# Ternary weight pieces shared between two engines, and TensorE's filler loads left out, in an eight-core FFN-attention-FFN kernel

## The chip, the cores and the metric

The kernel runs on the 8 NeuronCores of one Trainium2 chip, one batch element of 4096 rows of 1024 numbers on each core. The cores share no data. The metric is the device time in microseconds of the slowest core.

## The reference, cut to what matters

```python
# layer 0 (macaron)
x = x + 0.5 * ffn(layernorm(x), w_gate, w_up, w_down)
x = x + attn(layernorm(x), Wq1, bq1, Wk1, bk1, Wk2, bk2, Wproj, bproj)
x = x + 0.5 * ffn(layernorm(x), w_gate, w_up, w_down)

def weight_quant(w):               # one scale per matrix
    scale = 1.0 / clip(mean(abs(w)), 1e-05)
    return clip(round(w * scale), -1.0, 1.0) / scale

def ffn(x, w_gate, w_up, w_down):  # 1024 -> 4096 -> 1024
    gate = silu(act_quant(x) @ weight_quant(w_gate).T)
    up = act_quant(x) @ weight_quant(w_up).T
    return act_quant(gate * up) @ weight_quant(w_down).T

def attn(V, ...):                  # elementwise, with running sums over the rows
    K = exp(V @ Wk1.T + bk1);  Q = sigmoid(V @ Wq1.T + bq1)
    O_ar = cumsum(K * V) / (cumsum(K) + 1e-6) * Q
    ...
    return (O_ar + O_ma) @ Wproj.T + bproj
```

## The kernel before, in words

**Ternary weights.** The three FFN matrices (16 MB each in float32) are turned into matrices of -1, 0 and 1 in bf16, once, and kept in device memory (`sc_g`, `sc_u`, `sc_d`). `emit_tern_stream` does it one matrix after the other, in two passes each. The mean pass (`tern_mean`, `mean_piece`) loads 16 pieces of 128 x 2048 and ScalarE sums their absolute values (L237); `mean_finalize` makes a scale of it. The write pass (`tern_write_gu`, `tern_write_d`) loads the 16 pieces again, and `tern_piece` works on each: two DVE operations over 2048 elements scale and clamp it (L291, L294), then four times two operations over 512 elements add a large constant while converting to int32 (L301) and subtract it while converting to bf16 (L304). That rounds. POOL's queue then issues the store (L310).

Pieces go through four load buffers (`tpc`) and four store buffers (`tst`), chosen by `bsel`, the running number of the piece modulo 4. SP issues all piece loads (L231), in order, each when the last user of its buffer is done (`slotV`). A new mean pass on ScalarE starts when DVE has done all it was given up to there (`cV.wait(S)` in `tern_mean`).

**The main loop.** It takes 8 chunks of 512 rows. For each: the first FFN (`emit_ffn_rest`), attention (`emit_attn`), then the second FFN. The gate and up weights are loaded in slices by ScalarE's queue (`gu_load`, L549 and L551), the first two right before the matmuls of L602 and L607. Transposes come before the matmuls, rounded out of PSUM by DVE (L420, L425) or ScalarE (L436, L440) in turn.

**Attention's end.** The elementwise chain (`chain(th)`) is done for the two halves of a chunk, th = 0 and 1, in four lanes of two column blocks: lanes 0 and 1 on DVE, 2 and 3 on POOL with scans on DVE. `wproj_mms(th)` multiplies its result with Wproj on TensorE: four bias matmuls (L1022), then eight matmuls of 128x512 for each lane (L1037), which wait for the lane and for the lane's pair of weight blocks (`dAW`, loaded by POOL's queue, L734). `te_fill(n)` puts n weight loads of 128x128 without a matmul (L1013) into TensorE's queue: 140 at the start of a half, 50 ahead of each later lane's wait. `wproj_evac(th)` adds the result to the chunk on DVE (L1055). The order of emission, and so of each engine's queue, is: `chain(0)`, `wproj_mms(0)`, `chain(1)`, `wproj_evac(0)`, a part of the layer norm statistics, `wproj_mms(1)`, `wproj_evac(1)`, and then the second FFN's quantising and transposes.

Of the kernel before, what the change touches and what calls it, by code (L numbers as in the profile page):

```python
# [10 lines left out]
AF = mybir.ActivationFunctionType  # L11
ALU = mybir.AluOpType
# [28 lines left out]
def build_nc(L=4096, T=512):  # L41
# [21 lines left out]
    if DEBUG_ATTN:  # L63
# [20 lines left out]
    aq = poolb[:, 0:4096].rearrange("p (a b c) -> p a b c", a=TT, b=DC)  # L84
# [21 lines left out]
    qiV = qi32[:, 0:512]  # L106
    qiS = qi32[:, 512:1024]
# [30 lines left out]
    nm128_ap = smal[:, 187:188]  # L138
    dcol = smal[:, 143:144]
# [16 lines left out]
    cV = Sem(st, nc, "cV")  # L156
    cS = Sem(st, nc, "cS")
# [3 lines left out]
    V, S, TE, SY, G = nc.vector, nc.scalar, nc.tensor, nc.sync, nc.gpsimd  # L161
# [24 lines left out]
                           scalar1=-2.0, scalar2=-1.0,  # L186
                           op0=ALU.add, op1=ALU.mult))
    cV.wait(V)
    V.tensor_scalar(out=dcol, in0=t1[:, 0:1], scalar1=MAGIC, scalar2=None,
                    op0=ALU.mult)  # L190
    cV.inc(V.tensor_scalar(out=nm128_ap, in0=t1[:, 0:1], scalar1=-MAGIC,
                           scalar2=None, op0=ALU.mult))
    dB.inc(SY.dma_start(out=bsb[:, 0:DC],
                        in_=bq1.ap().rearrange("(j p) -> p j", p=128),
                        allow_slow_non_contiguous=True), 16)
    dB.inc(SY.dma_start(out=bsb[:, DC:2 * DC],
                        in_=bk1.ap().rearrange("(j p) -> p j", p=128),
                        allow_slow_non_contiguous=True), 16)
    dB.inc(SY.dma_start(out=bsb[:, 2 * DC:3 * DC],
                        in_=bk2.ap().rearrange("(j p) -> p j", p=128),  # L200
# [7 lines left out]
                           op0=ALU.mult))  # L208
    dX[0].inc(SY.dma_start(out=xsb[0][:, :, :],
                           in_=x_hbm.ap()[0:T, :]  # L210
# [8 lines left out]
    tw_state = {"idx": 0, "slotV": [None] * 4, "stgV": [None] * 4}  # L219

    def tern_dma_in(src_ap, pf):
        i = tw_state["idx"]
        tw_state["idx"] += 1
        bsel = i % 4
        buf = tpc[bsel][:, 0:pf]
        if tw_state["slotV"][bsel] is not None:
            sem_, n_ = tw_state["slotV"][bsel]
            SY.wait_ge(sem_.h, n_)
        else:
            cV.wait(SY)  # L230
        dTI[bsel].inc(SY.dma_start(out=buf, in_=src_ap), 16)  # L231
        return bsel, buf
# [53 lines left out]
    def tern_piece(src_ap, dst_ap, sw_slot, pf, osems, sw_wait=False):  # L286
        bsel, buf = tern_dma_in(src_ap, pf)
        sbf = tst[bsel][:, 0:pf]
        dTI[bsel].wait(V)
        cV.wait(V)  # L290
        cV.inc(V.tensor_scalar(out=buf, in0=buf, scalar1=sw_slot, scalar2=1.4375,  # L291
                               op0=ALU.mult, op1=ALU.min))
        cV.wait(V)
        cV.inc(V.tensor_scalar(out=buf, in0=buf, scalar1=-1.4375,  # L294
                               scalar2=None, op0=ALU.max))
        prev = tw_state["stgV"][bsel]
        if prev is not None:
            prev[0].wait(V, prev[1])
        for j0 in range(0, pf, 512):
            cV.wait(V)  # L300
            cV.inc(V.tensor_scalar(out=qiV[:, 0:512], in0=buf[:, j0:j0 + 512],  # L301
                                   scalar1=dcol, scalar2=None, op0=ALU.add))
            cV.wait(V)
            cV.inc(V.tensor_scalar(out=sbf[:, j0:j0 + 512], in0=qiV[:, 0:512],  # L304
                                   scalar1=nm128_ap, scalar2=None,
                                   op0=ALU.add))
        tw_state["slotV"][bsel] = (cV, cV.n)
        cV.wait(G)
        osem = osems[bsel]
        osem.inc(G.dma_start(out=dst_ap, in_=sbf), 16)  # L310
        tw_state["stgV"][bsel] = (osem, osem.n)

    def tern_write_gu(w_hbm, scratch, sw_slot, osems):
        for ob in range(8):
            for icg in range(2):
                src = bass.AP(w_hbm, icg * 4 * 128 * INNER + ob * 512,
                              [[INNER, 128], [128 * INNER, 4], [1, 512]])
                dst = bass.AP(scratch, ob * (128 * 8 * 512) + icg * 4 * 512,
                              [[8 * 512, 128], [512, 4], [1, 512]])
                tern_piece(src, dst, sw_slot, 2048, osems,  # L320
                           sw_wait=(ob == 0 and icg == 0))

    def tern_write_d(w_hbm, scratch, sw_slot, osems):
        for icg in range(8):
            for h2 in range(2):
                src = bass.AP(w_hbm, (icg * 4 + h2 * 2) * 128 * D,
                              [[D, 128], [128 * D, 2], [1, D]])
                dst = bass.AP(scratch, icg * (128 * 4 * 1024) + h2 * 2 * 1024,
                              [[4 * 1024, 128], [1024, 2], [1, 1024]])
                tern_piece(src, dst, sw_slot, 2048, osems,  # L330
                           sw_wait=(icg == 0 and h2 == 0))
# [388 lines left out]
    def emit_attn(c, xb, pre01_done=False):  # L720
# [8 lines left out]
        def aw_load(w_hbm, k):  # L729
            bs = k % 4  # L730
            G.wait_ge(cT.h, aw_arena_cT[bs])
            src = bass.AP(w_hbm, (k % 4) * 2 * 128 * D,
                          [[D, 128], [128 * D, 2], [1, D]])
            dAW[bs].inc(G.dma_start(  # L734
                out=awb[:, bs * 2048:(bs + 1) * 2048], in_=src), 16)

        def aw_tile(k, et):
            bs = (k // 2) % 4
            off = bs * 2048 + (k % 2) * 1024 + et * 128
            return awb[:, off:off + 128]  # L740
# [267 lines left out]
                cV.inc(V.tensor_copy(out=xnc, in_=xn2T[:, :, 512]))  # L1008
            return lane_done

        def te_fill(n):
            for _ in range(n):
                TE.ldweights(weights=aq[:, 0, 0, :])  # L1013

        def wproj_mms(th, lane_done):
            TE.wait_ge(cV.h, wp_evac_cV[th])
            TE.wait_ge(cS.h, proj_evac_cS[th])
            te_fill(140)
            TE.wait_ge(lane_done[0][0].h, lane_done[0][1])
            for tt in (th * 2, th * 2 + 1):  # L1020
                for eb in range(2):
                    TE.matmul(out=pb[th * 4 + (tt % 2) * 2 + eb][:, :],  # L1022
                              lhsT=onesrb[:, :],
                              rhs=bprow[:, eb * 512:(eb + 1) * 512],
                              start=True, stop=False)
            for dc in range(DC):
                kp = dc // 2
                bsel = kp % 4
                dAW[bsel].wait(TE)
                if dc % 2 == 0:  # L1030
                    if kp > 0:
                        te_fill(50)
                    TE.wait_ge(lane_done[kp][0].h, lane_done[kp][1])
                tl_ = None
                for tt in (th * 2, th * 2 + 1):
                    for eb in range(2):
                        tl_ = TE.matmul(  # L1037
                            out=pb[th * 4 + (tt % 2) * 2 + eb][:, :],
                            lhsT=OB_[:, dc, tt * 128:(tt + 1) * 128],
                            rhs=aw_tile(dc, 0)[:, 0:0 + 512] if False else  # L1040
                            awb[:, bsel * 2048 + (dc % 2) * 1024 + eb * 512:
                                bsel * 2048 + (dc % 2) * 1024 + (eb + 1) * 512],
                            start=False, stop=(dc == DC - 1))
                cT.inc(tl_)
                if dc % 2 == 1:
                    aw_arena_cT[bsel] = cT.n
                    if kp + 2 < 4:
                        aw_load(wpt, kp + 2)
# [24 lines left out]
        if DEBUG_ATTN and c == 0:  # L1073
# [3 lines left out]
                                 in_=pool[:, 8192:12296]), 16)  # L1077
# [9 lines left out]
        aw_load(wpt, 1)  # L1087
        lanes0 = chain(0)
        wproj_mms(0, lanes0)
        aw_load(wpt, 0)  # L1090
        aw_load(wpt, 1)
        lanes1 = chain(1)
        if DEBUG_ATTN and c == 0:
            cV.wait(SY)
            cS.wait(SY)
            for i_, ap_ in enumerate([pool[:, 4096:8192], pool[:, 12296:16392],
# [5 lines left out]
                                    in_=ap_), 16)  # L1102
            dDB.inc(SY.dma_start(out=bass.AP(dbgq, 0, [[4104, 128], [1, 4104]]),
                                in_=poolb[:, 4096:8200]), 16)
            dDB.inc(SY.dma_start(out=bass.AP(dbgq, 128 * 4104,
                                            [[4104, 128], [1, 4096]]),
                                in_=poolb[:, 8200:12296]), 16)
# [3 lines left out]
        wproj_evac(0)  # L1111
        ln_stats_part(xb, (0, 1))
        wproj_mms(1, lanes1)
        wproj_evac(1)

# [6 lines left out]
    for c in range(NCH):  # L1122
        xb = xsb[c % 2]
        if c + 1 < NCH:
            if c >= 1:
                dO.wait(SY, 16 * c)
            dX[(c + 1) % 2].inc(SY.dma_start(
                out=xsb[(c + 1) % 2][:, :, :],
                in_=x_hbm.ap()[(c + 1) * T:(c + 2) * T, :]
# [6 lines left out]
        if c + 1 < NCH:  # L1136
# [6 lines left out]
            out=y_hbm.ap()[c * T:(c + 1) * T, :].rearrange("(a p) d -> p a d",  # L1143
                                                           p=128),
            in_=xb[:, :, :]), 16)
# [29 lines left out]
```

## Time and profile before

| | us |
|---|---|
| timed runs | 6789.29 and 6901.66 (median 6845.48) |
| profiled execution | 6789.22 |
| its span on the slowest core (core 4) | 6788.2 |
| spans of the eight cores | 6708.1 to 6788.2 |
| mean granted TensorE clock of the eight cores | 0.794 to 0.800 of full speed |
| busy on core 4: TensorE, DVE, ScalarE, POOL | 3997.4, 2602.3, 1580.0, 489.5 |

Times in the rows further down are microseconds from the start of core 4's span. PE is TensorE's matmuls, PEld its weight loads, DVE is VectorE, ACT ScalarE, POOL GpSimd, SP the engine that only issues DMAs; ACTq is ScalarE's sequencer, which issues DMAs too. A granted clock of 1.00 is 2.4 GHz, 0.50 is 1.2 GHz.

### The profile page before, as it was taken

How to read it: one execution, taken by the hardware profiler on the slowest of the kernel's cores; microseconds unless marked ns; L12 is line 12 of the kernel's file. 1: busy time of each engine (PE TensorE's matmuls, PEld its weight loads, DVE VectorE, ACT ScalarE, POOL GpSimd, SP SyncE). 2: the span in 40 equal slices, each digit the busy share in tenths (PEclk: the TensorE clock that was granted, in tenths of full speed). 3: DMA queues.
4: the chain of work that ended last, by engine and by line, in shares of the span. 5: the costliest groups of instructions: out<-in, count | busy, mean ns of one | idle time of the engine just before them, and what ended most of it. 6: DMA issues, size and time to landing. Idle time of an engine off the chain costs nothing.

```text
span 6788.2 us, 61510 instructions; the slowest of 8 cores (6708.1 to 6788.2 us)
## 1 busy us (share of the span) xinstructions
PE 3997.4 (59%) x19026; PEld 2319.6 (34%) x23666; DVE 2602.3 (38%) x4295; ACT 1580.0 (23%) x2080; POOL 489.5 (7%) x505
## 2 busy tenths in 40 slices
PE   0006647576377745686376754686475763777457
PEld 0002333344333343334343343333333433333333
DVE  4555343331642244332532325422433315422352
ACT  2111221231131221322131321312213311312212
POOL 0000020001200020000200011000200002000200
PEclk6558868798689867898688877898687986898778
DMA  6784343235224252244233252243432352232522
GB/s 210 241 257 156 73 73 106 75 102 120 46 81 139 84 93 81 64 135 98 51 100 112 90 103 69 68 155 72 73 104 70 104 111 51 87 124 84 94 81 90
DMA packets 229245, 700.29 MB, mean 103 GB/s; under 512 B 22096, under 2 KB 22096, under 8 KB 224848
## 3 DMA queue, kind: packets, MB, share of 16 engines
q10 hardware_dynamic: 110592, 402.70, 19.0%
q0 software_dynamic: 76576, 159.41, 12.8%
q1 hardware_dynamic: 41776, 134.24, 6.4%
q8 instruction: 180, 2.95, 0.2%
q14 instruction: 121, 0.99, 0.1%
HBM read 788.55 MB, written 41.94 MB: 122 GB/s over the span
## 4 chain that ended last, share of the span: by engine, by line
PE 39%; DVE 23%; DMA 15%; ACT 13%; issue 7%; POOL 1%; DVEq 1%; ACTq 0%; SPq 0%; POOLq 0%
PE PB L602 11%; PE PB L607 10%; PE PB L684 9%; DMA sarena<-sc_d 8%; PE PB L754 4%; PE PB L403 4%; DVE pool L572 3%; ACT qi L436 2%; DMA sarena<-sc_u 2%; ACT poolb L440 2%; ACT pool L643 2%; DMA poolb<-wq1t 2%; DVE poolb L304 1%; DVE qi L301 1%; DVE smal L578 1%
## 5 line engine op out<-in xcount | busy, mean ns | idle before, releaser
L602 PE MATMUL PB<-sarena,poolb 128*128 128x512 bf16 x4096 | 1578.9, 385 | 358.8 <-DMA sarena<-sc_u 129.9
L607 PE MATMUL PB<-sarena,poolb 128*128 128x512 bf16 x4096 | 1577.9, 385 | 0.0
L684 PE MATMUL PB<-sarena,poolb 128*128 128x512 bf16 x4096 | 956.0, 391 | 228.6 <-DMA sarena<-sc_d 227.3
L403 PE MATMUL PB<-ident,pool 128*128 128x128 f32 x2144 | 496.6, 368 | 960.1 <-ACT pool L517 367.0
L572 DVE SCALAR_TENSOR_TENSOR pool<-PB,smal,pool 128x512 f32<-128x512 f32 x512 | 381.8, 746 | 1314.0 <-ACT pool L569 1314.0
L403 PEld LDWEIGHTS PB<-ident,pool 128*128 128x128 f32 x2144 | 379.1, 197 | 999.4 <-issue 997.6
L602 PEld LDWEIGHTS PB<-sarena,poolb 128*128 128x128 bf16 x4096 | 405.4, 99 | 921.8 <-issue 478.0
L684 PEld LDWEIGHTS PB<-sarena,poolb 128*128 128x128 bf16 x4096 | 396.2, 100 | 784.2 <-issue 374.1
L569 ACT ACTIVATE pool<-PB,smal 128x512 f32<-128x512 f32 x512 | 326.5, 684 | 1423.0 <-PE PB L607 1391.7
L607 PEld LDWEIGHTS PB<-sarena,poolb 128*128 128x128 bf16 x4096 | 405.3, 99 | 473.4 <-issue 28.7
L754 PE MATMUL PB<-poolb 128*128 128x256 bf16 x3072 | 401.1, 296 | 169.2 <-ACT pool L770 125.5
L697 DVE SCALAR_TENSOR_TENSOR xsb<-PB,smal,xsb 128x512 f32<-128x512 f32 x64 | 43.6, 744 | 1160.4 <-PE PB L684 1160.4
L420 DVE TENSOR_SCALAR qi<-PB,smal 128x512 int32<-128x512 f32 x320 | 240.1, 750 | 432.6 <-PE PB L406 418.2
L754 PEld LDWEIGHTS PB<-poolb 128*128 128x128 bf16 x3072 | 319.7, 106 | 250.8 <-issue 187.7
L1037 PE MATMUL PB<-poolb 128*128 128x512 bf16 x512 | 211.3, 588 | 325.5 <-issue 201.2
L578 DVE TENSOR_REDUCE smal<-pool 128x1 f32<-128x512 f32 x512 | 351.0, 686 | 55.0 <-DVE pool L572 2.7
L734 POOL DMA_DIRECT2D poolb<-wk1t x64 | 45.8, 720 | 4363.6 <-PE PB L684 4274.8
L1013 PEld LDWEIGHTS <-poolb 128*128 128x128 bf16 x4640 | 210.8, 101 | 188.9 <-issue 188.0
L436 ACT ACTIVATE qi<-PB,smal 128x512 int32<-128x512 f32 x320 | 220.1, 688 | 155.4 <-PE PB L406 135.0
L643 ACT ACTIVATE pool<-pool,smal 128x4096 f32<-128x4096 f32 x64 | 232.1, 3697 | 61.2 <-DVE smal L627 57.5
L406 PE MATMUL PB<-ident,pool 128*128 128x128 f32 x672 | 240.3, 358 | 0.0
L440 ACT ACTIVATE poolb<-qi,smal 128x512 bf16<-128x512 int32 x320 | 231.0, 722 | 30.3 <-ACT qi L436 0.7
(140 smaller groups left out, 3016.9 us busy)
## 6 DMA issues: line engine op xcount, KB each, us to landing
sarena<-sc_g ACTq DMA_DIRECT2D x256, 512.0 KB, 4.3
sarena<-sc_u ACTq DMA_DIRECT2D x256, 512.0 KB, 5.3
sarena<-sc_d ACTq DMA_DIRECT2D x256, 512.0 KB, 3.9
pool<-wgt SPq DMA_DIRECT2D x32, 1024.0 KB, 9.9
pool<-wut SPq DMA_DIRECT2D x32, 1024.0 KB, 8.9
pool<-wdt SPq DMA_DIRECT2D x32, 1024.0 KB, 10.2
poolb<-wk1t POOLq DMA_DIRECT2D x64, 512.0 KB, 8.1
poolb<-wq1t POOLq DMA_DIRECT2D x64, 512.0 KB, 8.0
```

The costliest lines, as they stand in the source:

```text
L403: TE.transpose(out=PB[:, b * 1024 + j * 128: b * 1024 + (j + 1) * 128], in_=s_, identity=ident[:, :])
L406: cT.inc(TE.transpose(out=PB[:, b * 1024 + (len(srcs) - 1) * 128: b * 1024 + len(srcs) * 128], in_=srcs[-1], identity=ident[:, :]))
L436: cS.inc(S.activation(out=qiS[:, 0:w_], in_=pt, func=AF.Identity, bias=dcol))
L440: cS.inc(S.add(out=dst, in_=qiS[:, 0:w_], add=nm128_ap))
L569: cS.inc(S.activation(out=sl, in_=pb[ttg * 4 + (tt % 2)][:, :], func=AF.Silu, scale=cg[:, tt:tt + 1]))
L572: cV.inc(V.scalar_tensor_tensor(out=hbuf[:, tt, ob_ * 512:(ob_ + 1) * 512], in0=pb[ttg * 4 + 2 + (tt % 2)][:, :], scalar=cu[:, tt:tt + 1], ...
L578: cV.inc(V.reduce_max(out=hpart[:, tt * 8 + ob_:tt * 8 + ob_ + 1], in_=hbuf[:, tt, ob_ * 512:(ob_ + 1) * 512], axis=AXX, apply_absolute_va ...
L602: TE.matmul(out=pb[ttg * 4 + (tt % 2)][:, :], lhsT=aq[:, tt, ic, :], rhs=gsl[:, bsel * 2048 + ic4 * 512: bsel * 2048 + (ic4 + 1) * 512], s ...
L607: tl_ = TE.matmul(out=pb[ttg * 4 + 2 + (tt % 2)][:, :], lhsT=aq[:, tt, ic, :], rhs=usl[:, bsel * 2048 + ic4 * 512: bsel * 2048 + (ic4 + 1) ...
L643: cS.inc(S.activation(out=hbuf[:, tt, :], in_=hbuf[:, tt, :], func=AF.Identity, scale=s2v[:, tt:tt + 1]))
L684: tl_ = TE.matmul(out=pb[tt * 2 + obk][:, :], lhsT=hq[:, tt, ic, :], rhs=dsl[:, bsel * 2048 + ic2 * 1024 + obk * 512: bsel * 2048 + ic2 * ...
L754: tl_ = TE.matmul(out=pb[et][:, 0:HT], lhsT=aw_tile(dc, et), rhs=xn2T[:, dc, rhs_off + th * HT: rhs_off + th * HT + HT], start=(dc == 0), ...
```

## The change

It has two parts. In `tern_piece`, pieces in odd buffers (every second one) have their eight 512-wide operations done by ScalarE, with an activation that adds the constant as its bias and an add; the two clamps stay on DVE. The waits for the store buffer, for the loads' buffer and for the store move with them to ScalarE's semaphore. In `wproj_mms`, `te_fill` and its calls are gone.

```diff
@@ tern_piece
         prev = tw_state["stgV"][bsel]
-        if prev is not None:
-            prev[0].wait(V, prev[1])
-        for j0 in range(0, pf, 512):
-            cV.wait(V)
-            cV.inc(V.tensor_scalar(out=qiV[:, 0:512], in0=buf[:, j0:j0 + 512],
-                                   scalar1=dcol, scalar2=None, op0=ALU.add))
...
-        tw_state["slotV"][bsel] = (cV, cV.n)
-        cV.wait(G)
+        on_s = bsel % 2 == 1
+        if on_s:
+            if prev is not None:
+                prev[0].wait(S, prev[1])
+            cV.wait(S)
+            for j0 in range(0, pf, 512):
+                cS.wait(S)
+                cS.inc(S.activation(out=qiS[:, 0:512], in_=buf[:, j0:j0 + 512],
+                                    func=AF.Identity, bias=dcol))
+                cS.wait(S)
+                cS.inc(S.add(out=sbf[:, j0:j0 + 512], in_=qiS[:, 0:512],
+                             add=nm128_ap))
+            tw_state["slotV"][bsel] = (cS, cS.n)
+            cS.wait(G)
+        else:
...
@@ emit_attn
-        def te_fill(n):
-            for _ in range(n):
-                TE.ldweights(weights=aq[:, 0, 0, :])
-
         def wproj_mms(th, lane_done):
             TE.wait_ge(cV.h, wp_evac_cV[th])
             TE.wait_ge(cS.h, proj_evac_cS[th])
-            te_fill(140)
             TE.wait_ge(lane_done[0][0].h, lane_done[0][1])
...
                 if dc % 2 == 0:
-                    if kp > 0:
-                        te_fill(50)
                     TE.wait_ge(lane_done[kp][0].h, lane_done[kp][1])
```

How the pieces stand in DVE's queue: from the last operations of the first piece of the first write pass. Before:

```order
L301 TENSOR_SCALAR qi<-pool,smal 128x512
L304 TENSOR_SCALAR poolb<-qi,smal 128x512
L291 TENSOR_SCALAR pool<-pool,smal 128x2048
L294 TENSOR_SCALAR pool<-pool 128x2048
L301 TENSOR_SCALAR qi<-pool,smal 128x512
L304 TENSOR_SCALAR poolb<-qi,smal 128x512
```

Now (L316 and L321 are the former L301 and L304):

```order
L316 TENSOR_SCALAR qi<-pool,smal 128x512
L321 TENSOR_SCALAR poolb<-qi,smal 128x512
L291 TENSOR_SCALAR pool<-pool,smal 128x2048
L294 TENSOR_SCALAR pool<-pool 128x2048
L291 TENSOR_SCALAR pool<-pool,smal 128x2048
L294 TENSOR_SCALAR pool<-pool 128x2048
L316 TENSOR_SCALAR qi<-pool,smal 128x512
L321 TENSOR_SCALAR poolb<-qi,smal 128x512
```

The second piece has only its two clamps left here; the third piece's clamps follow at once.

ScalarE's queue between its last quantising of chunk 0's input and the first FFN weight loads. Before:

```order
L440 ACTIVATE poolb<-qi,smal 128x512
L237 ACTIVATE pool,smal<-pool 128x2048 x48
L549 DMA sarena<-sc_g 128x2048
L551 DMA sarena<-sc_u 128x2048
```

Now the 48 sums stand in three groups of 16, each followed by 64 operations of a write pass; these are the end of the last group and the loads (L567 and L569 are the former L549 and L551):

```order
L304 ACTIVATE qi<-pool,smal 128x512
L307 ACTIVATE poolb<-qi,smal 128x512
L304 ACTIVATE qi<-pool,smal 128x512
L307 ACTIVATE poolb<-qi,smal 128x512
L567 DMA sarena<-sc_g 128x2048
L569 DMA sarena<-sc_u 128x2048
```

The loads have moved behind the last odd piece of the third write pass.

TensorE's queue at the output projection of chunk 0, both halves. Before:

```order
L1013 LDWEIGHTS poolb x140
L1022 MATMUL PB<-bprow,onesrb 128x512 x4
L1037 MATMUL PB<-poolb 128x512 x8
L1013 LDWEIGHTS poolb x50
L1037 MATMUL PB<-poolb 128x512 x8
L1013 LDWEIGHTS poolb x50
L1037 MATMUL PB<-poolb 128x512 x8
L1013 LDWEIGHTS poolb x50
L1037 MATMUL PB<-poolb 128x512 x8
L1013 LDWEIGHTS poolb x140
```

Now:

```order
L1035 MATMUL PB<-bprow,onesrb 128x512 x4
L1048 MATMUL PB<-poolb 128x512 x32
L1035 MATMUL PB<-bprow,onesrb 128x512 x4
L1048 MATMUL PB<-poolb 128x512 x32
```

The matmuls and their order are the same; the weight loads between them are gone.

## Rows read from the trace of the kernel before

**Rows 1.** The page: the span, and the DMA line in 40 slices.

```profile
span 6788.2 us, 61510 instructions; the slowest of 8 cores (6708.1 to 6788.2 us)
...
DMA  6784343235224252244233252243432352232522
```

**Rows 2.** Windows (busy us of PE, PEld, DVE, ACT, POOL; PEclk, DMA share, GB/s): mean, write.

```profile
47.00:101.00 54.00, 0.19 (x2) 0.11 (x2) 0.17 (x1) 32.03 (x32) 0.00 (x0) 0.50 0.99 332
103.00:223.00 120.00, 0.00 (x0) 0.00 (x0) 102.45 (x162) 0.19 (x1) 14.54 (x15) 0.50 0.70 215
```

**Rows 3.** Timeline (start, duration) of the second piece in the first write pass.

```profile
110.67 1.28 DVE L291 TENSOR_SCALAR pool<-pool,smal 128x2048 f32<-128x2048 f32 x1
...
113.40 0.49 DVE L301 TENSOR_SCALAR qi<-pool,smal 128x512 int32<-128x512 f32 x1
...
118.15 1.29 DVE L291 TENSOR_SCALAR pool<-pool,smal 128x2048 f32<-128x2048 f32 x1
```

**Rows 4.** Line 1055's own view: what DVE waited for before it, us and times.

```profile
  PE PB L1037: 46.0, 8
```

**Rows 5.** Timeline, second half's projection: chunk 0, chunk 5 (two rows), last chunk (two).

```profile
1023.79 2.39 PEld L1013 LDWEIGHTS <-poolb 128*128 128x128 bf16 x50 [9.96 <-issue]
1026.13 3.59 PE L1037 MATMUL PB<-poolb 128*128 128x512 bf16 x8 [11.39 <-issue]
...
1031.33 1.90 PE L1037 MATMUL PB<-poolb 128*128 128x512 bf16 x8 [1.61 <-issue]
1033.34 1.29 DVE L1055 TENSOR_TENSOR xsb<-PB,xsb 128x512 f32<-128x512 f32 x2 [5.05 <-PE PB L1037]
...
4931.61 3.59 PE L1037 MATMUL PB<-poolb 128*128 128x512 bf16 x8 [1.75 <-issue]
4935.31 1.29 DVE L1055 TENSOR_TENSOR xsb<-PB,xsb 128x512 f32<-128x512 f32 x2 [7.24 <-PE PB L1037]
...
6496.18 2.39 PEld L1013 LDWEIGHTS <-poolb 128*128 128x128 bf16 x50 [11.60 <-issue]
...
6505.61 0.69 DVE L1055 TENSOR_TENSOR xsb<-PB,xsb 128x512 f32<-128x512 f32 x1 [6.58 <-PE PB L1037]
```

**Rows 6.** Timeline of ScalarE at the end of the first transposes.

```profile
44.60 0.72 ACT L440 ACTIVATE poolb<-qi,smal 128x512 bf16<-128x512 int32 x1
...
45.42 0.69 ACT L436 ACTIVATE qi<-PB,smal 128x512 int32<-128x512 f32 x1
...
46.20 0.72 ACT L440 ACTIVATE poolb<-qi,smal 128x512 bf16<-128x512 int32 x1
```

**Rows 7.** DMA issues (KB each, median us to landing): first write pass, last write pass.

```profile
pool<-wgt SPq DMA_DIRECT2D x12, 1024.0 KB, 5.9
...
sarena<-sc_u ACTq DMA_DIRECT2D x2, 512.0 KB, 16.4
```

**Rows 8.** Timeline: end of the third write pass; start of chunk 0's second FFN.

```profile
567.84 0.48 DVE L304 TENSOR_SCALAR poolb<-qi,smal 128x512 bf16<-128x512 int32 x1
...
569.25 0.58 PE L602 MATMUL PB<-sarena,poolb 128*128 128x512 bf16 x1 [121.19 <-DVE smal L535]
...
1059.60 0.72 ACT L440 ACTIVATE poolb<-qi,smal 128x512 bf16<-128x512 int32 x1
...
1067.24 0.59 PE L602 MATMUL PB<-sarena,poolb 128*128 128x512 bf16 x1 [8.89 <-DMA sarena<-sc_u]
...
1071.44 0.38 PE L602 MATMUL PB<-sarena,poolb 128*128 128x512 bf16 x1
```

**Rows 9.** Timeline: the 140 fills of the first half and the bias matmuls.

```profile
925.14 6.11 PEld L1013 LDWEIGHTS <-poolb 128*128 128x128 bf16 x140 [2.06 <-issue]
...
948.92 1.86 PE L1022 MATMUL PB<-bprow,onesrb 1*128 1x512 bf16 x4 [25.55 <-DVE poolb L941]
```

**Rows 10.** Windows, columns as in rows 2: the two fill stretches of chunk 0.

```profile
1023.80:1026.10 2.30, 0.00 (x0) 2.30 (x50) 2.30 (x4) 0.00 (x0) 0.00 (x0) 0.50 0.87 162
1029.60:1031.30 1.70, 0.13 (x1) 1.70 (x42) 0.00 (x0) 0.00 (x0) 0.00 (x0) 0.75 0.00 0
```

More of the change, by code:

```diff
@@ L296, in tern_piece @@
         prev = tw_state["stgV"][bsel]
-        if prev is not None:
-            prev[0].wait(V, prev[1])
-        for j0 in range(0, pf, 512):
-            cV.wait(V)
-            cV.inc(V.tensor_scalar(out=qiV[:, 0:512], in0=buf[:, j0:j0 + 512],
-                                   scalar1=dcol, scalar2=None, op0=ALU.add))
[L303 to L306, printed above, removed]
-        tw_state["slotV"][bsel] = (cV, cV.n)
-        cV.wait(G)
+        on_s = bsel % 2 == 1
[13 more added lines that the diff above has]
+        else:
+            if prev is not None:
+                prev[0].wait(V, prev[1])
+            for j0 in range(0, pf, 512):
+                cV.wait(V)
+                cV.inc(V.tensor_scalar(out=qiV[:, 0:512],
+                                       in0=buf[:, j0:j0 + 512],
+                                       scalar1=dcol, scalar2=None,
+                                       op0=ALU.add))
+                cV.wait(V)
+                cV.inc(V.tensor_scalar(out=sbf[:, j0:j0 + 512],
+                                       in0=qiV[:, 0:512],
+                                       scalar1=nm128_ap, scalar2=None,
+                                       op0=ALU.add))
+            tw_state["slotV"][bsel] = (cV, cV.n)
+            cV.wait(G)
         osem = osems[bsel]
```

## The prediction

> **What bounds the kernel now.** I read the page first [rows 1]: the slowest core spans 6788.2 us, and the DMA line has its highest digits in the first three of its 40 slices. That is the preparation of the ternary FFN weights, which ends with the first FFN matmul at 569 us [rows 8]. Then I took windows over it [rows 2]: while a mean is formed the DMA engines are 99% busy (332 GB/s) and ScalarE a good half; while a matrix is written out, DVE is busy 102.45 of 120 us, ScalarE 0.19 of 120 us and DMA 70%. So the three mean passes are bound by the weight loads, the three write passes by DVE. Third, the timeline inside a write pass [rows 3]: one piece runs from 110.67 to 118.15, that is 7.48 us, with gaps of about 0.1 us only between dependent operations. Sixteen pieces make 119.6 us, three passes 359 us, all of it ahead of the first FFN matmul and so on the path.
>
> Fourth, the attention's output projection. It is done in two halves for each of 8 chunks. In the first half nobody waits for TensorE, since `wproj_evac(0)` stands behind `chain(1)` on DVE. In the second half DVE does wait for it: 46.0 us over 8 chunks [rows 4], with nothing else in between. In chunk 0 [rows 5] TensorE starts 50 fill loads at 1023.79, when the third weight pair has landed, eight matmuls at 1026.13, then fills again, the last eight matmuls at 1031.33, and DVE resumes at 1033.34. Those fills are in DVE's wait.
>
> **Part A, odd pieces to ScalarE.** Of an odd piece DVE keeps the two 2048-wide clamps: from 110.67 to 113.40 [rows 3], 2.73 us. The eight 512-wide operations leave it. A pair of pieces then costs DVE 7.48 + 2.73 = 10.2 us in place of 14.96. On ScalarE the eight operations are the same two forms that it runs in the transposes: 0.69 (int32 out) and 0.72 (bf16 out), start to start 0.82 and 0.78 [rows 6], so 4 x 1.60 = 6.4 us a pair, well under 10.2. Its source is SBUF here and PSUM there, which no row of this form shows; L440 reads SBUF at 0.72, and even 1.0 us an operation would leave ScalarE at 8.8 us, below DVE. The moved work has cover until 10.2 us; what is left over is the tail: the last piece of a pass is an odd one, and its 6.4 us on ScalarE come after DVE's last clamp. Floor of a pass: 8 x 10.2 + 6.4 = 88.0 us, 31.6 less than now.
>
> What is late next are the loads. SP issues them in order, each when its buffer is free, so with the change they leave in twos: an even piece ends 7.5 us into its pair, the odd one before it about a microsecond earlier. An odd buffer is held 2.7 + 6.4 = 9.1 us of a 20.4 us cycle (four buffers, two pairs), so its load may take 11.3 us before DVE waits. Loads land in 5.9 us in this window, the slowest transfers of the last pass in 16.4 us [rows 7]. As to throughput, a pair moves 3.15 MB (two loads of 1 MB and two stores of half that): at 332 GB/s [rows 2] 9.5 us. The 70% share over 120 us is 84 us of DMA work a pass, 10.5 us a pair if none of it shrinks. So loads and DVE come out nearly level. Ends for a pair: 10.2 (DVE alone) and (9.1 + 16.4) / 2 = 12.75 (every load as late as the slowest seen). The nearest row is the 84 us, and it holds loads that this pass does not itself await, so I take 10.6. A pass: 8 x 10.6 + 6.4 = 91.2 us, 28.4 saved; three passes 85 us (range 34 to 95).
>
> The Trainium skill weighs in here: DMA: Bandwidth & Descriptors, section Specifications, gives a core some 358 GB/s when both cores of a memory share it. By that a pair needs 8.8 us by estimate and DMA is never late, where the trace's 332 GB/s gives 9.5; the pass would then be the 88.0 us floor.
>
> The mean passes stay: the loads of their first pieces still leave while the last three pieces are worked on. What A adds is one thing. ScalarE's queue also issues the first FFN loads. Today they stand right behind the last sum and have landed long before the third write pass ends; the first matmul (569.25) follows DVE's last rounding operation (567.84 + 0.48) by 0.9 us [rows 8]. Now they stand behind 64 operations, the last odd piece among them. In the second FFN the same step is exposed: the last quantising operation starts at 1059.60 and ends 0.72 later, the matmul starts at 1067.24: 6.9 us. Cost: 6.9 - 0.9 = 6 us, once. A gives 85 - 6 = 79 us (28 to 89).
>
> **Part B, fills removed.** 4640 weight loads go. The 140 before the bias matmuls are hidden in every half: they start at 925.14 and take 6.11 us, and the matmul they precede starts at 948.92, after DVE [rows 9]. The 50 before the second pair end before DVE's lane too. The 50 before the third and fourth pair of the second half are on the path. From the start of the third pair's fills to DVE: chunk 0 9.55 us, last chunk 9.43 us [rows 5]; the eight are 9.6, 11.1, 11.2, 9.2, 9.3, 11.4, 9.3, 9.4, together 80.4 us (the first and the last stand in the rows). Without fills 16 matmuls follow one another. At half clock eight start every 0.427 us, 3.4 us, and the slow group in chunk 5 reaches DVE after 4935.31 - 4931.61 = 3.70 us [rows 5], so 7.1 us; at full clock the group took 1033.34 - 1031.33 = 2.01 us, 16 would need some 3.7 us. All cold: 80.4 - 57 = 23.5 us saved. All warm: 50.7, but no more than the 46.0 that DVE waits. In between: in the FFN cold dense matmuls from 1067.24 are full speed by 1071.44, after about 4 us [rows 8], while the first block of fills runs at a granted 0.50 and the second at 0.75 [rows 10]. A run of 6.8 us may catch the rise in its last third; I take 6.6 us a chunk, 52.8 us in all: 27.6 us saved.
>
> What the fills gave is the other side of this. In chunk 0 the clock rose during the second block of them and the last group ran in 1.90 us; in chunk 5 it did not (3.59). TensorE: Matmul & The Clock Gate in the Trainium skill, section HAM oscillation, wants the array kept dense because every gap starts cold again. Taken against this change it says that the fills earn the warm last group and that all 16 matmuls now run cold: 23.5 us in place of 27.6. The trace agrees in part: both levels occur after the same fills. Everything after is untouched: between this projection and the next transposes TensorE waits for DVE and ScalarE in any case.
>
> **Sum.** 79 + 28 = 107 us. The profiled execution took 6789.2 us: 6682 us. That execution is at the lower of the two timed runs (6789.29, 6901.66; median 6845.48). Ends of the sum: 89 + 46 = 135 saved (6654), 28 + 20 = 48 saved (6741).
>
> **Rivals.** First, the loads are the bound of the new write pass: for it, 70% busy already and the loads leaving in twos; against it, landings of 5.9 us against 11.3 allowed. A pair then costs 12.75, a pass 108.4, A saves 34 - 6 = 28: 6789 - 56 = 6733 us.
>
> Second, the slower side: DVE and ScalarE end up in series. SP's queue is strictly in order, so the free even buffer waits behind the odd one still on ScalarE; if that coupling starves DVE, a pair costs 7.48 + 2.73 + 6.4 = 16.6 us, a pass 132.8, and A loses 3 x 13.2 + 6 = 46 against B's 28: 6807 us. It decides from a load time of 16.6 x 2 - 9.1 = 24 us, above every row.
>
> Third, the fills hid something: DVE's 46 us end on the weights' landing instead. For it, the waits are put down to TensorE in either case; against it, the fill itself already waits for that landing. B is nothing: 6710 us.
>
> Fourth, both parts reach their ends (loads never late, clock rising early): 6654 us.
>
> **How the numbers follow.** Forecast 0.70, first rival 0.12, second 0.04, third 0.08, fourth 0.06. The sum's own range is 6654 to 6741. The upper end of the range given is 6770, since the kernel's runs reach above the profiled one and the second rival lies there. About 2% is what a measurement of this kernel can tell from no change, 136 us: 6653 from the profiled execution, but 6709 from the median. The forecast of 1.6% stays within it. Faster 0.25 is the fourth case and the part of the forecast in which the kernel before is measured nearer its median; slower 0.03 is the second case and a bad spread; same 0.72.
>
> **What would show it.** In the changed profile: DVE pieces alternating 7.5 and 2.7 us; ScalarE some 51 us busy in a write pass; passes of 88 to 95 us; DVE gaps ending on SP's loads would mean the first rival, ScalarE at over 9 us a piece the second. First FFN matmul near 569 - 79 = 490 us. DVE's wait at `wproj_evac(1)` down from 46.0 to about 18 us, granted clock 0.50 for most of these 16 matmuls. The prediction is wrong if the first matmul is later than 541 us (A under 28), if the waits fall by less than 20 us, or if any stage after 569 us grows.

## The result, and the profile after

The changed kernel takes 6708.63 us in the median of 11 runs (6694.25 to 6763.46), the kernel before 6824.94 in the median of 10. The ratio, taken from the runs in which neither half of the chip was slowed by a lower clock, is 0.9854, with a 95% interval of 0.9809 to 0.9899: 1.5% faster. The forecast was 6682 us, 1.6% faster.

The page of the changed kernel, its first lines and the DMA line. They answer to [rows 1].

```profile
span 6702.7 us, 56894 instructions; the slowest of 8 cores (6617.2 to 6702.7 us)
...
DMA  7992522325324333225224252243332352242522
```

The span of the slowest core is 85 us shorter, the mean of the eight 96 us (6751.2 to 6654.8); which core is slowest differs from run to run. The DMA line starts with 7, 9, 9 and then drops: the preparation of the weights is shorter and denser. Windows over its three write passes on the slowest core say the same, columns as in [rows 2]:

```profile
105.90:197.60 91.70, 0.00 (x0) 0.00 (x0) 71.32 (x96) 46.17 (x65) 11.94 (x15) 0.50 0.92 271
252.40:348.90 96.50, 0.00 (x0) 0.00 (x0) 71.29 (x96) 46.22 (x65) 10.84 (x15) 0.50 0.90 260
403.20:495.10 91.90, 0.00 (x0) 0.00 (x0) 71.67 (x98) 46.20 (x64) 12.05 (x15) 0.50 0.84 263
```

Passes of 92 to 96 us in place of 120; DVE busy 71 us in each in place of 102, ScalarE 46, and the DMA share up from 0.70 to between 0.84 and 0.92. The timeline of the second and third piece, to be held against [rows 3]:

```profile
113.33 1.28 DVE L291 TENSOR_SCALAR pool<-pool,smal 128x2048 f32<-128x2048 f32 x1
...
116.06 1.28 DVE L291 TENSOR_SCALAR pool<-pool,smal 128x2048 f32<-128x2048 f32 x1
116.10 0.72 ACT L304 ACTIVATE qi<-pool,smal 128x512 int32<-128x512 f32 x1 [13.18 <-DVE pool L294]
116.91 0.72 ACT L307 ACTIVATE poolb<-qi,smal 128x512 bf16<-128x512 int32 x1
...
123.53 1.28 DVE L291 TENSOR_SCALAR pool<-pool,smal 128x2048 f32<-128x2048 f32 x1
```

DVE steps 2.73 us over the odd piece and 7.47 over the even one, and ScalarE starts 0.04 us after DVE has let go. The form that no row had shown, int32 written from a source in SBUF, takes 0.72 us. What DVE waited for before its first clamp (line 291's own view) is new; the first two of its lines:

```profile
  DMA pool<-wut: 8.8, 4
  DMA pool<-wgt: 4.0, 3
```

The end of the third pass, against [rows 8]: ScalarE's last operation, the first FFN load, the first matmul.

```profile
494.35 0.72 ACT L307 ACTIVATE poolb<-qi,smal 128x512 bf16<-128x512 int32 x1
494.87 0.35 ACTq L567 DMA_DIRECT2D sarena<-sc_g  x1
...
503.24 0.59 PE L620 MATMUL PB<-sarena,poolb 128*128 128x512 bf16 x1 [100.44 <-DMA sarena<-sc_u]
```

The projection's second half in chunk 0, against [rows 5], and what DVE waited for in all eight chunks, against [rows 4] (line 1066 was 1055):

```profile
952.81 1.48 POOL L752 DMA_DIRECT2D poolb<-wpt  x2
...
958.35 5.67 PE L1048 MATMUL PB<-poolb 128*128 128x512 bf16 x16 [9.23 <-DMA poolb<-wpt]
964.13 1.29 DVE L1066 TENSOR_TENSOR xsb<-PB,xsb 128x512 f32<-128x512 f32 x2 [1.38 <-PE PB L1048]
```

```profile
  PE PB L1048: 13.0, 8
```

Sixteen matmuls in 5.67 us, and DVE's wait down from 46.0 to 13.0 us. The two slowest cores are not the same one; in the mean of the eight cores the wait falls from 50.4 to 11.6 us.

To see where the rest of the time went I cut each core's trace at the starts and ends of its groups of matmuls and summed the pieces over the chunks. Means of the eight cores, in us; the kernels with one part each are the first two experiments below.

| stretch | before | odd pieces only | no fills only | both |
|---|---|---|---|---|
| start to first FFN matmul | 569.9 | 502.4 | 569.8 | 501.0 |
| second halves' projection, first bias matmul to last matmul | 285.4 | 289.0 | 247.3 | 246.4 |
| second FFN, gate and up matmuls, first to last | 965.9 | 967.9 | 976.2 | 973.1 |
| everything else | 4930.0 | 4939.1 | 4934.0 | 4934.3 |
| mean span | 6751.2 | 6698.4 | 6727.3 | 6654.8 |

The first row is part A, 69 us. The second is part B, 39 us. The third goes against the change: 7 to 10 us are lost in the second FFN, in the columns without fills. The fourth moves by up to 10 us from run to run without any of these edits touching it.

### The profile page after: what moved, and what is told of

Same layout as the page of the kernel before. It is cut to its first block, busy times and chain, and to the rows that moved or that the text cites. A ratio compares the mean times of both kernels' runs of the same rounds, so it can differ in the third digit from the quotient of the medians.

```text
span 6702.7 us, 56894 instructions; the slowest of 8 cores (6617.2 to 6702.7 us)
## 1 busy us (share of the span) xinstructions
PE 3979.1 (59%) x19026; PEld 2099.2 (31%) x19026; DVE 2508.9 (37%) x4103; ACT 1718.3 (26%) x2272; POOL 479.0 (7%) x505
## 4 chain that ended last, share of the span: by engine, by line
PE 40%; DVE 21%; DMA 17%; ACT 14%; issue 7%; POOL 1%; DVEq 1%; ACTq 0%; SPq 0%; POOLq 0%
PE PB L620 11%; PE PB L625 11%; PE PB L702 9%; DMA sarena<-sc_d 8%; PE PB L772 4%; PE PB L421 4%; DMA sarena<-sc_u 3%; DVE pool L590 3%; ACT qi L454 2%; ACT pool L661 2%; ACT poolb L458 2%; DMA poolb<-wq1t 2%; DVE smal L596 1%; ACT pool L587 1%; DMA pool<-wut 1%
## 5 line engine op out<-in xcount | busy, mean ns | idle before, releaser
L421 PE MATMUL PB<-ident,pool 128*128 128x128 f32 x2144 | 483.5, 361 | 966.8 <-ACT pool L535 367.2
L1035 PE MATMUL PB<-bprow,onesrb 1*128 1x512 bf16 x64 | 29.8, 615 | 356.2 <-DVE poolb L959 356.2
L424 PE MATMUL PB<-ident,pool 128*128 128x128 f32 x672 | 235.4, 350 | 0.0
## 6 DMA issues: line engine op xcount, KB each, us to landing
pool<-wgt SPq DMA_DIRECT2D x32, 1024.0 KB, 10.6
```

The source lines that it names most:

```text
L421: TE.transpose(out=PB[:, b * 1024 + j * 128: b * 1024 + (j + 1) * 128], in_=s_, identity=ident[:, :])
```

## The experiments

**One part each.** `a_only` has the new `tern_piece` and the old `wproj_mms`, `b_only` the reverse; `hidden_gone` is the kernel before with only the fills that I held to be on the path:

```diff
         def wproj_mms(th, lane_done):
...
-            te_fill(140)
...
                 if dc % 2 == 0:
-                    if kp > 0:
+                    if th == 1 and kp > 1:
                         te_fill(50)
```

> Only the odd pieces move to ScalarE, all fills stay. Theory (the parts are independent and add up): first FFN matmul near 501 us (569.9 before, mean of cores), write passes near 94 us, the second halves' projection (bias matmuls to last matmul, summed over 8 chunks) unchanged at 285 us, the whole 65 to 72 us shorter, ratio near 0.990. Rival (all of the gain comes from this part, the rest being noise): 95 us shorter, ratio near 0.986.

> Only the fills go, the pieces stay on DVE. Theory: first FFN matmul at 570 us as before, the second halves' projection 246 us against 285, the whole 35 to 39 us shorter, ratio near 0.995; DVE's wait before line 1055's counterpart falls from 46 to about 13 us. Rival (the recorded term, 28 us): 257 us. Second rival (the wait moves to the landing of the weights): no shorter than 275 us.

> The kernel before with 3840 of its 4640 fills gone: only the two blocks of 50 ahead of the third and fourth weight pair of each second half stay. Theory (only these 800 are on the path): second halves' projection stays at 285 us, no change of time beyond noise, and the last group of matmuls still starts at full clock in most chunks. Rival (the hidden fills prepare the clock or delay TensorE too): it falls by 5 us or more, or the last groups all turn slow, 285 plus 8 x 0.7 = 291 us.

Measured: `a_only` 0.990 (0.9873 to 0.9927), `b_only` 0.9948 (0.9926 to 0.997). Multiplied that is 0.985, the ratio of both together: within these intervals the parts are independent and add up, and the rival of `a_only` is out. In time, 1.0% and 0.5% of some 6807 us, 68 and 35 us. The projection of `a_only` was not quite unchanged: it takes 289 us in place of 285, and DVE's wait before line 1055's counterpart is 54.2 us in place of 50.4 (mean of cores). The last group of matmuls began at a granted clock of 1.00 in 9 of its 64 cases (8 chunks, 8 cores), in 24 before. In `b_only` DVE waits 15.5 us where it waited 46.0, and the projection takes 247 us: the recorded 257 was too cautious, the wait did not move to the weights' landing. `hidden_gone` took 6822.59 us in its one run, no less than the kernel before (median 6806.63). Four of its cores ran at a granted clock of 0.81 for 129 to 184 us each (last section); the mean span of the other four, 0 to 3, is 6750.7 us, against 6749.6 for the same cores before. Its projection stays at 284.5 us and DVE still waits as before:

```profile
1020.98 2.39 PEld L1013 LDWEIGHTS <-poolb 128*128 128x128 bf16 x50 [9.81 <-issue]
1023.32 3.59 PE L1036 MATMUL PB<-poolb 128*128 128x512 bf16 x8 [11.51 <-issue]
...
1032.24 2.48 DVE L1054 TENSOR_TENSOR xsb<-PB,xsb 128x512 f32<-128x512 f32 x4 [6.62 <-PE PB L1036]
```

So 3840 of 4640 fills cost nothing and gave nothing, and the gain is that of the other 800. One part of what I expected here was wrong: the last group does not start at full clock in most chunks, but in 19 of 64 cases (24 of 64 before).

**What bounds the new write pass.** `even_on_s` swaps the roles, so that a pass ends with a piece of DVE's:

```diff
-        on_s = bsel % 2 == 1
+        on_s = bsel % 2 == 0
```

> The changed kernel with the even pieces on ScalarE in place of the odd ones, so that the last piece of a pass is DVE's. Theory (the 6.4 us tail is real and DVE is the bound within the pass): a pass falls from 93.7 to 88 us or below, and the first FFN matmul comes about 16 us earlier, at 485 us. Rival (loads and stores set the pass): the pass stays within 2 us of 93.7.

`double_store` stores each piece once more, to memory that nobody reads (`sc_x`, new):

```diff
         osem.inc(G.dma_start(out=dst_ap, in_=sbf), 16)
+        osem.inc(G.dma_start(out=sc_x.ap()[tw_state["idx"] - 1], in_=sbf), 16)
```

> The changed kernel with each piece stored a second time to spare memory: a pair moves 4.2 MB in place of 3.15. Theory (DVE bounds the pass, with transfers close behind): at some 330 GB/s a pair now needs 12.7 us, the pass grows by 8 x 2.1 = 17 to 25 us, to 111 to 119 us. Rival (transfers have room to spare): the pass stays under 98 us.

The last write pass of the first and the first of the second, each on its slowest core, columns as in [rows 2]:

```profile
387.40:472.60 85.20, 0.00 (x0) 0.00 (x0) 71.33 (x96) 46.35 (x64) 10.95 (x15) 0.50 0.90 279
```

```profile
103.60:211.70 108.10, 0.00 (x0) 0.00 (x0) 71.36 (x96) 46.23 (x65) 24.08 (x30) 0.50 0.97 294
```

With the even pieces on ScalarE a pass takes 83.7 us (mean of cores and passes), 10 less, and the first matmul comes at 479.5 us: the tail was real. The mean span is 6625.7 us, 29 less than the changed kernel's. The swap gave 30 us less in passes but 22 at the first matmul, since the two mean passes between grew by 3.9 and 2.5 us and the gap before the first matmul by 1.6. The loads of the next pass, which used to get ahead in the tail, now have no tail to use; that this is why they grew was not tested by itself. With doubled stores a pass takes 111, 112 and 105 us at a DMA share of 0.97 and 294 GB/s, 16 us longer on average: 1 MB more in a pair costs 2 us. Both theories hold in the main, the second at the lower edge of its 111 to 119 us. DVE's work sets the pass as it stands, at 8 x 10.2 + 6.4 = 88 us. The 6 us between 88 and 93.7 are DVE's waits for the pieces to land: 5.6 us a pass in the changed kernel, 2.3 with the even pieces on ScalarE, 19.6 with doubled stores (mean of cores and passes).

**The first FFN loads.** `gu_on_sp` takes the first four of them from ScalarE's queue; the wait for the gate and up stores moves to SP with them:

```diff
-            S.wait_ge(cT.h, gu_arena_cT[bs])
+            Q = SY if c == 0 and first_ffn and k < 2 else S
+            Q.wait_ge(cT.h, gu_arena_cT[bs])
...
-            dGU[bs].inc(S.dma_start(
+            dGU[bs].inc(Q.dma_start(
```

> The changed kernel with the first four FFN weight loads of chunk 0 issued by SP, behind the last piece load, and not by ScalarE behind the last odd piece. Theory (the first matmul waits because the loads stand behind ScalarE's work): the gap from the end of the last pass to the first matmul falls from 8.5 us to about 1 us, the first matmul is at 493 to 495 us. Rival (the gap is contention with the last stores and the next chunk's input): it stays above 5 us.

The gap fell from 8.5 to 6.4 us only. SP's queue on core 4, and how long transfers from there took from issue to landing (last column, window of 455 to 510 us):

```profile
470.14 0.47 SPq L1140 DMA_DIRECT2D xsb<-x  x1
471.47 0.34 SPq L569 DMA_DIRECT2D sarena<-sc_g  x1
```

```profile
xsb<-x SPq DMA_DIRECT2D x1, 2048.0 KB, 21.6
sarena<-sc_g SPq DMA_DIRECT2D x2, 512.0 KB, 22.2
sarena<-sc_u SPq DMA_DIRECT2D x2, 512.0 KB, 26.0
```

In the changed kernel the first of these loads left at 489.0 us on the same core, 17.5 us later. The first up slice, which the first matmul needs, landed at 497.0 us there and at 497.1 here, behind 2 MB of the next chunk's input and the last stores. The rival was right: at the end of the third pass there is a backlog of transfers, and the place in ScalarE's queue is the smaller part. Four cores of this run also had a lower clock for 386 to 664 us (last section), which is why its whole time, 6746.85 us, says nothing.

**The projection's weights.** All four weight pairs are still in place when the second half starts. `no_reload` uses them:

```diff
                 if dc % 2 == 1:
                     aw_arena_cT[bsel] = cT.n
-                    if kp + 2 < 4:
+                    if th == 0 and kp + 2 < 4:
                         aw_load(wpt, kp + 2)
...
         wproj_mms(0, lanes0)
-        aw_load(wpt, 0)
-        aw_load(wpt, 1)
         lanes1 = chain(1)
```

> The changed kernel without the second loading of the projection weights: they are still in place from the first half. Theory (what is left of DVE's wait, 13 us, and TensorE's late start come from POOL issuing the third and fourth load behind its lanes): DVE's wait falls from 13 us to 0 and the second halves' projection from 246 to below 200 us; the whole 13 to 18 us shorter. Rival (DVE is not waiting for that): DVE's wait stays above 8 us.

DVE does not wait for TensorE before line 1066 at all any more, and the projection takes 177 us. From the first half's bias matmuls to the second FFN's first matmul it is 24.6 us less a core (916.0 to 891.4), as the 13 us of waiting and POOL's issuing would have it. Of this 6.6 us arrive in the mean span, 6648.2 against 6654.8; the stretch between the first FFN and the first bias matmul, which the edit does not touch, was 14 us longer in this run than in the changed kernel's (2046 against 2031; the other kernels lie between 2025 and 2042). Six cores of this run were also at a clock of 0.81 for 61 to 393 us. TensorE was busy for 118 us of it in the mean of the eight cores, and a fifth of that, 22 us, is the most that it can have cost (an estimate). But on the two cores without it, 6 and 7, no gain shows in the span either. One run cannot say more; `combined` below can.

**The loss in the second FFN.** Counting the starts of gate and up matmuls that follow one another at 0.427 us (within some 4 ns), half clock, in the second FFN: about 75 a core before, 73 in `a_only`, 72 in `hidden_gone`, but 116 in `b_only`, 101 with both, 106 in `no_reload`. 26 more at 0.21 us each are 5.5 of the 7 us lost. The granted clock says the same: in this stretch it was 0.50 for 33.9 us a core before, 46.9 with both and 53.5 in `b_only`. Half of the difference, 6.5 and 9.8 us, is nearly the whole loss of 7 and 10. Here is chunk 2 of the changed kernel on its slowest core, from the first matmul on:

```profile
2548.10:2553.20 5.10, 5.10 (x13) 1.80 (x14) 0.00 (x0) 0.00 (x0) 0.00 (x0) 0.50 0.22 92
2553.20:2566.50 13.30, 11.35 (x53) 4.96 (x51) 2.96 (x5) 3.32 (x5) 0.00 (x0) 1.00 0.25 80
2566.50:2570.50 4.00, 3.92 (x11) 1.48 (x12) 2.51 (x4) 0.61 (x1) 0.00 (x0) 0.57 0.69 229
2570.50:2580.00 9.50, 9.50 (x46) 4.32 (x45) 0.27 (x1) 1.06 (x2) 0.00 (x0) 1.00 0.38 117
```

The clock rises after some 5 us, and 18 us in it falls to half once more for about 3.4 us. The timeline shows what TensorE did just before: it waited 2.03 us for DVE, and 0.2 us after the wait the matmuls are slow.

```profile
2564.17 0.38 PE L625 MATMUL PB<-sarena,poolb 128*128 128x512 bf16 x1
2566.58 0.38 PE L620 MATMUL PB<-sarena,poolb 128*128 128x512 bf16 x1 [2.03 <-DVE smal L596]
2566.79 0.59 PE L625 MATMUL PB<-sarena,poolb 128*128 128x512 bf16 x1
2567.18 0.63 PE L620 MATMUL PB<-sarena,poolb 128*128 128x512 bf16 x1
```

Chunk 0 of the kernel before, on its slowest core, does not fall again:

```profile
1067.20:1072.30 5.10, 5.06 (x14) 1.85 (x15) 0.00 (x0) 0.00 (x0) 0.00 (x0) 0.59 0.16 63
1072.30:1085.60 13.30, 11.27 (x53) 5.02 (x52) 3.34 (x5) 3.71 (x5) 0.00 (x0) 1.00 0.24 79
1085.60:1089.60 4.00, 4.00 (x20) 1.76 (x19) 2.12 (x4) 0.22 (x1) 0.00 (x0) 1.00 0.62 116
```

But the kernel before can do it too, with all its fills in place; this is its chunk 2 on core 1:

```profile
2604.40:2610.10 5.70, 5.70 (x14) 1.98 (x15) 0.00 (x0) 0.00 (x0) 0.00 (x0) 0.50 0.09 35
2610.10:2623.70 13.60, 11.57 (x54) 5.10 (x53) 3.44 (x5) 3.90 (x5) 0.00 (x0) 1.00 0.21 77
2623.70:2627.20 3.50, 3.50 (x10) 1.23 (x9) 2.03 (x3) 0.03 (x1) 0.00 (x0) 0.51 0.81 281
```

The same wait of 2.0 us, 15 to 17 us in, stands in all 64 second FFNs of either kernel. The second fall comes in 8 of them before, in 31 with both parts and in 39 in `b_only`. What goes with it is how late the clock first rose. In the six kernels whose cores never ran at 0.81 (384 second FFNs), it fell again in all 152 where the rise came 4.6 us or more after the first matmul, and in 3 of the 232 where it came earlier.

Is it the loads themselves that leave the clock in a better state? `fill_after` puts some where they cost nothing:

```diff
         wproj_mms(1, lanes1)
+        te_fill(100)
         wproj_evac(1)
```

> The changed kernel with 100 fill loads behind the last matmul of each second half's projection, where TensorE then waits some 18 us for other engines, so off the path. In all three kernels without fills on the path the second FFN's gate and up matmuls (first to last, summed over 8 chunks, mean of cores) take 973 to 978 us, with them 966 to 970, and the difference is matmuls at half clock (101 to 116 a core against 72 to 75). Theory (weight loads shortly before leave the clock in a better state): back to 965 to 968 us and about 75 slow matmuls, projection still 246 us, the whole 6 to 9 us shorter. Rival (it is where the matmuls fall in time, not the loads): 973 us and over 95 slow matmuls stay.

No: 975.7 us, 102 slow matmuls, and a second fall in 31 of 64 cases as without them. Its time, 6720.18 us, is no better either, though four of its cores ran at 0.81 for 75 to 188 us. So the loss goes with timing: without fills on the path the clock rises late more often, and TensorE's wait for DVE then more often ends in a fall. Why the rise comes late more often stays open; the fills' effect on the clock in the projection and the mere moment at which later work starts were not separated.

**All together.** `combined` has the even pieces on ScalarE, the weights loaded once, no fills, the first FFN loads on SP, and the next chunk's input behind these; `combined_fill` adds the 100 loads of `fill_after`.

```diff
         gu_load(0)
         gu_load(1)
+        if c == 0 and first_ffn:
+            x_load(1)
```

> Even pieces on ScalarE, the projection weights not loaded a second time, no fills, the first FFN loads of chunk 0 on SP's queue and the next chunk's input behind them. Theory (each gain stands by itself): first FFN matmul at 473 to 478 us (501 in the changed kernel, 479.5 with the even pieces alone, whose last 10 us were a backlog of transfers), 24 us less between the first half's bias matmuls and the second FFN, mean span near 6605 us, ratio to the kernel before 0.977 to 0.982. Rival (transfers take back what is gained: weights and input later collide): ratio above 0.984.

> The same with 100 fill loads behind each second half's projection. If loads restore the clock: 6 to 9 us below it in the second FFN's gate and up stretch (965 us); if not, the same time within 3 us.

`combined` takes 6644.16 us in the median of 6 runs (6633.82 to 6662.50), ratio 0.9778 (0.9748 to 0.9807) to the kernel before. It is faster than both kernels. The mean span is 6614.4 us, and 6600.9 over cores 4 to 7, which never ran at 0.81 as the other four did for 192 to 274 us; expected was 6605. The first matmul of its slowest core follows DVE at once, and the last write pass is DVE's floor:

```profile
381.10:463.10 82.00, 0.00 (x0) 0.00 (x0) 71.40 (x96) 46.22 (x64) 11.00 (x15) 0.50 0.90 283
```

```profile
464.03 0.59 PE L624 MATMUL PB<-sarena,poolb 128*128 128x512 bf16 x1 [83.33 <-DVE smal L554]
```

The mean over the cores is 470.4 us, earlier than the 473 to 478 expected: with the input behind them, the loads land before DVE is done, and the gap to the first matmul is 1.0 us. The second FFN's stretch is the longest of all, 982.8 us (33 us of it a core at 0.81), with a second fall of the clock in 45 of 64 cases. `combined_fill` is no better (0.9827, 0.9774 to 0.9880), and its second FFN's stretch, 981.5 us, is 1.3 us shorter and not 6 to 9; the fills bring nothing here, as in `fill_after`.

## Why the prediction was right

The result lies 27 us above the predicted 6682 and in the range; the forecast of faster, but under 2%, held. The 27 us are for the most part the base: I subtracted 107 us from a profiled execution of 6789.2 us, and the kernel before has a median of 6824.94. What was saved is 96 us in the mean span and 116 between the medians. By its steps:

- *Odd pieces on ScalarE.* The pair at 10.2 us of DVE is in the trace, and ScalarE's 6.4 us a pair too, of which it is busy 5.8 (46 us a pass, where I had written 51). The pass was put at 91.2 us, between 88.0 and 108.4; it took 93.7 in the mean of cores and passes. The taken 10.6 us a pair should have been 10.9: DVE waited for a load about three times a pass. Three passes gave 78 us in place of 85.
- *The tail and the first FFN loads.* The tail of 6.4 us showed in `even_on_s`. The step to the first matmul was put at 6 us more and took 7.5. The size was nearly right, the reason only in part: `gu_on_sp` shows that transfers waiting for one another make most of it. The rest of part A is about 1 us lost in each of the two later mean passes. In all 69 us in place of 79, `a_only` by itself 68.
- *Fills that are hidden.* Shown by `hidden_gone`: without these 3840 the projection takes 284.5 us in place of 285.4.
- *Fills on the path.* Put at 27.6 us; the projection became 39 us shorter. From the first of the 16 matmuls to DVE 5.8 us (958.35 to 964.13), where I took 6.6 and called 7.1 the case in which all run cold. That makes 6 us of the 11. The clock did better without the fills than I took: it is high at the start of the last group or rises within it in all 64 cases, and the group takes 2.33 us in the mean; with the fills that was so in 42 of 64, and the group took 2.92 us. The rest of the difference is the core I read: on the other seven, DVE waited 46.8 to 53.5 us before line 1055, on core 4 only 46.0. On core 4 the last group was fast in five of eight chunks, on all cores in 24 of 64.
- *Nothing after is touched.* This step failed, and with it one of my own signs of being wrong was met, a stage after 569 us that grows. The second FFN's gate and up matmuls take 7 us more (10 in `b_only`), because more of them run at half clock. I had weighed what the clock does within the projection and not what it does behind it. Net, part B is the 35 us of `b_only`.
- *The rivals.* Late loads (6733 us) are there in small, 6 us a pass and not 20; pushed on by doubled stores they take over. The series of DVE and ScalarE did not come: ScalarE waits for DVE, never the reverse. The third rival fell with DVE's wait of 13 us. For the clock I had cited TensorE: Matmul & The Clock Gate in the Trainium skill, section HAM oscillation, by which a wait for data sends the array back to the low clock. The trace agrees as far as the last group without fills begins at 0.50 in 58 of 64 cases. That all 16 matmuls would then run cold, the rival that I made of it, did not come. In the second FFN the fall does stand behind a wait, of 2.0 us, but the same wait is there in the cases without a fall, and in the kernel before.

The two errors, 10 us too much for A and some 7 too little for B, partly cancelled. Within B two more did: 11 us too little for the projection against 7 to 10 lost in the second FFN. That the sum came out so close is in part luck.

## What to carry to other kernels

Moving every second unit of work to an idle engine gives what the busy engine is relieved of, less the tail: let the last unit be that of the engine that is done first, and look at what the next stage's loads did in the time that goes. Filler work for the clock has to be counted on the path first: of these 4640 loads 800 were in a wait of 46 us, and none bought what it cost; the matmuls alone raised the clock more often than matmuls with fills between them. Before trimming a wait for a transfer, ask whether the data are already there. And when a stage is made shorter, look at the clock in the stages behind it: a short wait that cost only itself can now cost a fall of the clock too.

## What the runs showed of the hardware

The granted clock fell to half at the end of a wait of TensorE of only 2.0 us, between long runs of dense matmuls, for about 3.4 us. The same wait passed without a fall in 56 of 64 second FFNs before and in 33 of 64 after; in the kernels that never ran at 0.81 it always fell where it had first risen 4.6 us or more after the first matmul.

Weight loads did not hold the clock up: behind 50 of them the last group began at 1.00 in 24 of 64 cases. Sixteen matmuls of 128x512 in a row, without fills, ended at 1.00 in 64 of 64.

In six of the twelve profiles some cores ran matmuls at a granted clock of 0.81, neither of the two levels, for 61 to 664 us each, always in pairs (0 and 1, 2 and 3, 4 and 5, 6 and 7) and from the same moment within a pair. In `gu_on_sp` cores 0 and 1 did so in three chunks, from 531 us on, and cores 2 and 3 from 4689 us on, while core 4 ran at 1.00. What sets it off no run here shows. Windows of core 0 and of core 4 in the first gate and up stretch, matmuls counted in the second column:

```profile
520.00:600.00 80.00, 79.06 (x300) 31.95 (x301) 25.63 (x37) 10.81 (x18) 0.00 (x0) 0.82 0.37 125
```

```profile
520.00:600.00 80.00, 75.71 (x343) 33.40 (x349) 27.81 (x40) 12.77 (x20) 0.00 (x0) 1.00 0.44 140
```

Stores and loads together reached 294 GB/s at a DMA share of 0.97 in `double_store`, where loads alone reached 332 at 0.99 [rows 2].
